# Choice, flag and mask for one tile at a time, and recurrent products in half arrays, in a two-layer kernel with top-k dropping

## The reference

```python
# first layer, main branch
s = silu(einsum('bsh,ih->bsi', xn, w_gate))            # i: 1376
k = int(0.5 * I)                                       # 688
_, idx = top_k(-abs(s), k)                             # the 688 smallest |s| of a token
s = s.at[rows, idx].set(0.0)
s = s * einsum('bsh,ih->bsi', xn, w_up)
s = einsum('bsi,hi->bsh', s, w_down)
# first layer, gate branch: weights quantized to -1, 0, 1 by 0.7 of the row's mean |w|
g = silu(xn @ q_weight.T + bias)

# second layer, main branch: width 64, feed forward 256, depth 4
h = einsum('blv,dv->bld', xn, Win) + bin
for l in range(4):
    y = silu(layernorm(h, ln1_w, ln1_b))
    y = sconv(y, phz, lc)          # y_t = Re(sum_j p^j x_{t-j} + lc p^(t+1)), one complex p per channel
    h = h + y * sc_lin
    y = layernorm(h, ln2_w, ln2_b)
    h = h + silu(y @ w1.T + b1) @ w2.T + b2
s = layernorm(h, lnl_w, lnl_b) @ Wout.T + bout
# second layer, gate branch: x @ W.T plus 16 experts of rank 16, weighted
```

## Time and profile before

| | |
|---|---|
| time, median of 3 runs | 786.28 us (783.88, 789.82, 786.28) |
| the profiled execution | 782.56 us |
| its span in the trace | 780.6 us |
| TensorE busy | 665.8 us, 85% |
| VectorE busy | 513.9 us, 66% |
| ScalarE busy | 324.8 us, 42% |
| GpSimd busy | 241.5 us, 31% |
| mean granted TensorE clock | 0.927 |

### The profile page before, as it was taken

One profiled execution on the slowest core, in us unless ns is written; L12 is line 12 of the kernel. 1 busy time (PEld: TensorE's weight loads), 2 busy tenths in 40 slices (PEclk: granted clock), 3 DMA queues, 4 the chain that ended last, 5 costly groups with the idle time before them and its releaser, 6 DMA issues. The chain is left out here.

```text
span 780.6 us, 8884 instructions
## 1 busy us (share of the span) xinstructions
PE 665.8 (85%) x2724; PEld 475.7 (61%) x2724; DVE 513.9 (66%) x885; ACT 324.8 (42%) x537; POOL 241.5 (31%) x351
## 2 busy tenths in 40 slices
PE   2975898998998998998998987865979699596887
PEld 2764787887887887887887873743434244233443
DVE  6688596585685775865966862947472844727627
ACT  5467285184283373472672562112124133151320
POOL 1000001010010010010010063883346576685756
PEclk9997999999999999999999997985999789799889
DMA  7711001102002002002001080010000000000005
GB/s 265 245 45 55 0 1 46 36 1 78 3 0 81 0 0 81 0 0 81 0 0 55 2 283 28 0 42 0 15 0 13 0 0 13 0 0 13 0 0 216
DMA packets 19209, 33.16 MB, mean 42 GB/s; under 512 B 5008, under 2 KB 5520, under 8 KB 19184
## 3 DMA queue, kind: packets, MB, share of 16 engines
q1 hardware_dynamic: 19184, 32.87, 12.5%
HBM read 25.52 MB, written 7.34 MB: 42 GB/s over the span
## 5 line engine op out<-in xcount | busy, mean ns | idle before, releaser
L743 DVE TENSOR_SCALAR_CACHE_REDUCE junk_d<-k_buf,cand 128x1376 int8<-128x1376 f32 x56 | 91.8, 1640 | 0.3
L582 ACT ACTIVATE junk_a<-k_buf,cand 128x1376 int8<-128x1376 f32 x56 | 80.5, 1437 | 0.7
L979 PE MATMUL ps_a<-wd_hi,zt_hi 128*128 128x512 f32 (+1 forms) x176 | 72.0, 409 | 1.3 <-DVE zt_lo L856 1.0
L502 POOL TENSOR_TENSOR xres<-xres,gate 128x512 f32<-128x512 f32 x12 | 23.5, 1959 | 159.4 <-DVE gate L863 159.4
L954 PE MATMUL ps_a<-wg_hi,xt_hi 128*128 128x512 f32 (+1 forms) x192 | 54.9, 397 | 20.6 <-DVE gate L863 15.7
L979 PE MATMUL ps_a<-wd_hi,zt_lo 128*128 128x512 f32 (+1 forms) x176 | 69.1, 393 | 0.0
L979 PE MATMUL ps_a<-wd_lo,zt_hi 128*128 128x512 f32 (+1 forms) x176 | 69.0, 392 | 0.0
L563 ACT ACTIVATE s_buf<-ps_a 128x1376 f32<-128x1376 f32 x16 | 21.1, 1320 | 110.9 <-DVE m_buf L848 57.5
L1561 PE MATMUL ps_t<-arena 128*128 128x512 f32 x128 | 65.7, 644 | 0.0
L954 PEld LDWEIGHTS ps_a<-wg_hi,xt_hi 128*128 128x128 f32 x192 | 36.3, 201 | 28.6 <-DVE gate L863 14.2
L954 PE MATMUL ps_a<-wg_hi,xt_lo 128*128 128x512 f32 (+1 forms) x192 | 53.3, 388 | 0.0
(11 more groups left out here) (197 smaller groups left out, 1463.9 us busy)
## 6 DMA issues: line engine op xcount, KB each, us to landing
xin<-in_x SPq DMA_DIRECT2D x8, 512.0 KB, 4.0
xres<-in_x SPq DMA_DIRECT2D x8, 512.0 KB, 3.8
out<-arena SPq DMA_DIRECT2D x16, 256.0 KB, 2.3
x_scratch<-xres SPq DMA_DIRECT2D x6, 512.0 KB, 3.0
arena<-x_scratch SPq DMA_DIRECT2D x3, 1024.0 KB, 11.7
m_buf<-in_wd_t SPq DMA_DIRECT2D x3, 512.0 KB, 4.7
m_buf<-in_wg_t SPq DMA_DIRECT2D x2, 688.0 KB, 8.4
k_buf<-in_wg_t SPq DMA_DIRECT2D x2, 688.0 KB, 10.8
```

The lines of the kernel that those rows point to most:

```text
L502: pool.tensor_tensor(row, xres[:, t, :], gate2[:, t, :], ALU.add).then_inc(x1_ready, 1)
L582: act.activation(junk_a[:], k_buf[:, 1, :], ACT.Sign, bias=c, scale=-1.0, accum_out=below[:, 1:2]).then_inc(act_step, 1)
L743: dve.tensor_scalar(junk_d[:], k_buf[:, 0, :], c, -float(DROP), ALU.is_lt, ALU.add, accum_out=e).then_inc(cnt_dve, 1)
L979: last = pe.matmul(ps_a[:, t, :], zs, ws[0:rows, c, :], start=(c == 0 and n == 0), stop=(c == CHUNKS - 1 and n == 2))
```

## The change

Three things change together.

- **By tile.** `choose`, the flag's sum, the load of it, `exact_choice` and `mask` are done for one tile at a time. A choice is eleven steps on one column or 8 columns. The step that added two flags is gone; VectorE loads the summed flag itself. GpSimd does a residual and a sum, and again a residual and a sum.
- **Order on VectorE at a pair's end.** Before: `xt_low` 0, `largest_under` 1, `down_gate` 1, choice of both, `q_bias`, `xt_low` 1, flag, masks of both. Now: choice 0, `xt_low` 0, `down_gate` 1, `largest_under` 1, `q_bias`, mask 0, choice 1, `xt_low` 1; mask 1 stands behind the first two search steps of the next pair, ahead of its first `product`.
- **Second layer.** The padded arrays are gone: `win`, `w1`, `w2`, `wout` hold the weights alone, `w1` and `wout` once for each half of the partitions. Up and output products read 64 rows (sequence b's); `down_unit` and the `win` product write 64 rows of the output, one sequence each. Units go sequence by sequence (b = u % 2), in another order in `layer`, and the first up products of the second half stand ahead of the last down products of the first. `centered` is gone from VectorE: ScalarE squares straight from the bank and then copies to `xc`. The output tiles go in another order (`OUT`).

```diff
-PICKS = 12
+PICKS = 11
...
-                def residual(p, resident=False):
-
-                    for t in range(2):
-                        if t == 0:
-                            pool.wait_ge(x_res, 16 * p)
-                        pool.wait_ge(down_out, 2 * (p - 1) + t + 1)
-                        row = x1[:, 2 * (p - 1) + t, :] if resident else xres[:, t, :]
-                        pool.tensor_tensor(row, xres[:, t, :], gate2[:, t, :], ALU.add).then_inc(x1_ready, 1)
...
+                def residual(p, t, resident=False):
+
+                    if t == 0:
+                        pool.wait_ge(x_res, 16 * p)
+                    pool.wait_ge(down_out, 2 * (p - 1) + t + 1)
+                    row = x1[:, 2 * (p - 1) + t, :] if resident else xres[:, t, :]
+                    pool.tensor_tensor(row, xres[:, t, :], gate2[:, t, :], ALU.add).then_inc(x1_ready, 1)
+
+                def check_sum(p, t):
+
+                    pool.wait_ge(picked, PICKS * (2 * p + t + 1))
                     settled(pool, pool_passed)
-                    pool.partition_all_reduce(bad_all[:], bad[:], P, RADD).then_inc(bad_sum, 1)
+                    pool.partition_all_reduce(bad_all[:, t:t + 1], bad[:, t:t + 1], P, RADD).then_inc(bad_sum, 1)
...
-                check_sum(0)
+                check_sum(0, 0)
+                check_sum(0, 1)
                 with pool.Fori(1, PAIRS - 1) as p:
                     root(p + 1)
-                    residual(p)
-                    check_sum(p)
-
-                pool.wait_ge(up_done, TILES)
-                pool.memset(win, 0.0).then_inc(win_zero, 1)
+                    for t in range(2):
+                        residual(p, t)
+                        check_sum(p, t)
+
                 tables_start(pool)
...
-                residual(PAIRS - 1, resident=True)
-                check_sum(PAIRS - 1)
+                for t in range(2):
+                    residual(PAIRS - 1, t, resident=True)
+                    check_sum(PAIRS - 1, t)
                 tables_powers(pool, 0, 3, DOUBLINGS)
                 tables_powers(pool, 1, 0, DOUBLINGS - 1)
-                residual(PAIRS, resident=True)
+                for t in range(2):
+                    residual(PAIRS, t, resident=True)
...
-                    between()
-                    dve.wait_ge(bad_sum, p + 1)
-                    step(dve.tensor_tensor(bad_int[:, 0:1], bad_all[:, 0:1], bad_all[:, 1:2], ALU.add))
+
+                def mask(p, t):
+
+                    dve.wait_ge(bad_sum, 2 * p + t + 1)
                     settled(dve, dve_passed)
-                    failed = dve.value_load(bad_int[0:1, 0:1], min_val=0, max_val=2 * P)
+                    failed = dve.value_load(bad_all[0:1, t:t + 1].bitcast(I32), min_val=0, max_val=0x44000000)
                     with dve.If(failed > 0):
-                        exact_choice()
+                        exact_choice(t)
+                    dve.wait_ge(z_ready, 2 * p + t + 1)
+                    dve.scalar_tensor_tensor(out=m_buf[:, t, 0:INNER], in0=k_buf[:, t, :],
+                                             scalar=tau[:, t:t + 1], in1=s_buf[:, t, :],
+                                             op0=ALU.is_gt, op1=ALU.mult).then_inc(mask_ready, 1)
...
                     halve(p, 1)
+                    if back:
+                        mask(p - 1, 1)
                     product(p, 0)
...
+                    choose(p, 0)
                     if ahead:
                         xt_low(p + 1, 0)
-                    largest_under(p, 1, back)
                     if back:
                         down_gate(p, 1)
-
-                    def meanwhile():
-                        if first:
-                            dve.wait_ge(bias_in, 16)
-                        for t in range(2):
-                            q_bias(p, t, back)
-                        if ahead:
-                            xt_low(p + 1, 1)
-
-                    choose(p, meanwhile)
-                    mask(p)
+                    largest_under(p, 1, back)
+                    if first:
+                        dve.wait_ge(bias_in, 16)
+                    for t in range(2):
+                        q_bias(p, t, back)
+                    mask(p, 0)
+                    choose(p, 1)
+                    if ahead:
+                        xt_low(p + 1, 1)
...
                 def squares(q, c):
-                    act.wait_ge(ln_xc, 2 * q + c + 1)
-                    act.activation(sq[:, cs(c)], xc[:, cs(c)], ACT.Square).then_inc(ln_sq, 1)
+                    act.wait_ge(ln_cent, 2 * q + c + 1)
+                    act.activation(sq[:, cs(c)], bank1[c], ACT.Square).then_inc(ln_sq, 1)
+                    act.activation(xc[:, cs(c)], bank1[c], ACT.Copy).then_inc(ln_xc, 1)
...
-                        for b in range(BATCH):
-                            for k in range(KH):
-                                last = pe.matmul(bank1[c], win[:, b, k, :],
+                        for k in range(KH):
+                            for b in range(BATCH):
+                                last = pe.matmul(bank1[c][b * DIM:(b + 1) * DIM, :], win[:, k, :],
                                                  xt[:, k, b * SEQ + c * NB:b * SEQ + (c + 1) * NB],
-                                                 start=(b == 0 and k == 0), stop=(b == 1 and k == KH - 1))
+                                                 start=(k == 0), stop=(k == KH - 1))
...
-                    pe.matmul(bankx[u % 2], w1[:, b, m * P:(m + 1) * P], y[:, cs(c)],
+                    pe.matmul(bankx[u % 2], w1[rows, m * P:(m + 1) * P], y[rows, cs(c)],
                               start=True, stop=True).then_inc(f_full, 1)
...
-                    last = pe.matmul(bank1[c], w2[:, b, m, :], hs[:, u, :], start=(u == 0), stop=(u == 3))
+                    last = pe.matmul(bank1[c][b * DIM:(b + 1) * DIM, :], w2[:, m, :], hs[:, u, :],
+                                     start=(m == 0), stop=(m == 1))
```

More of the change, by code:

```diff
@@ L795, in choose @@
[L795 removed]
+                    rank_t, tau_t, above_t, bad_t = (x[:, t:t + 1] for x in (rank, tau, above, bad))
+                    pick_t, top_t = pick[:, t, :], top8[:, t, :]
+                    dve.wait_ge(at_ready, 2 * p + t + 1)
+                    dve.wait_ge(top_ready, 2 * p + t + 1)
+                    step(dve.tensor_scalar(rank_t, at_most[:, t:t + 1], 0.5, 0.25, ALU.mult, ALU.add))
+                    step(dve.tensor_scalar(pick_t, iota8[:], rank_t, None, ALU.subtract))
@@ L1150, in mixture_kernel @@
             FF = 2 * 4
-            OUT = [4 * g + j for g in ORDER for j in range(4)]
+            OUT = [8 * b + j for j in range(8) for b in range(BATCH)]
             def on_pool(m):
```

183 lines of the change are left out of this document (81 added, 102 removed).

## The result

The changed kernel takes 793.3 us in the median of 18 runs (787.08 to 798.72), the kernel before 785.15 (779.32 to 790.06): a ratio of 1.0096, 95% interval 1.0071 to 1.0121. It is slower by 1%, which is clear of the noise, and 801 was forecast: slower by 2%. The profiled execution took 790.37 us, its span is 788.5, 7.9 more than before.

The account below looks back on a forecast made before the run. TensorE was taken to bound the first half, delayed by waits for down_gate. 782.56 us + 27 for the first layer - 12 for the second = 797.6, with 3.7 to the median 801; range 787 to 819.

Parts of the forecast that it names:

- +18: End of the first layer, bound by GpSimd: 120.7 us behind the last pair's start against 102.7, through added code changes.
- +2.0 a pair: First layer's loop: two sums for one delay the up product; a pair goes from 56.4 to 58.4 us, five periods +10.
- before the second pair, down_gate ahead: First layer's start: the first pair's xt_low comes 1.8 us later, the next pair's waits of 2.22 and 0.3 go; -0.7.
- feed forward of four layers: Second layer: half arrays partly overlap, second half bound by ScalarE; -1.8 us a layer, -7 in all.
- win products: Second layer: 16 passes of the second half, 9.08 us, take nine steps, 5.1 us; -4.
- last norm and outputs: Second layer: squares from PSUM take the 0.7 us copy out of the chain only in the last norm; -0.7.
- start of block b: Second layer's start: w1, w2 and wout no longer cleared, which stood beside the wait for VectorE's norms; no gain counted.
- (1): Rival, second layer: the array halves do not overlap, or drains eat the gain; +14, 815 us; chance 0.22.
- (2): Rival, GpSimd in the first layer: change back costs little or is not between sum and second residual; 757 us; chance 0.05.
- (3): Rival: code changes at their short end, 6.1 us, TensorE's own path binds, all of the overlap; 791 us; chance 0.18.
- The drain: Second layer: tiling mode changes about six times a layer, each may drain TensorE; 1.6 us a layer, a reservation.
- The naive reading of down_gate: down_gate alone moved ahead: 2.6 us wait and 1 us low clock go in six pairs, nothing replaces them; -21, 764 us.

## Why the prediction was right and wrong

The direction and the mechanism were right: a change back to plain code between the first sum and the second residual, the wait of the up product, the longer end of the first layer, the gain of the half arrays. What failed is the size of the two terms of the first layer that decide. "+18" for its end measured +14.0: the change to the sum was put at 7.1 us (6.9 at the end), "the longest of the three", and took 5.8 to 6.4 in pairs 1 to 7. "+2.0 a pair" measured +1.4: the 0.4 a pair added because VectorE would lose its lead did not arise. These two make 7.2 of the 7.7 us by which the sum, 15.6 over the span of before, exceeds the measured 7.9. The other five terms miss by 0.4 to 2.4 us each and nearly cancel, and that they do is luck. Each term, with what the two traces give:

| term | predicted | measured |
|---|---|---|
| before the second pair, down_gate ahead | -0.7 | -3.1 |
| five periods | +10 | +6.8 |
| end of the first layer | +18 | +14.0 |
| feed forward of four layers | -7 | -6.1 |
| win products | -4 | -5.4 |
| last norm and outputs | -0.7 | -0.3 |
| start of block b | 0 | +2.0 |
| together | +15.6 | +7.9 |

**The second pair** (-0.7). I charged xt_low of the first pair 1.8 us for the choice ahead of it. It came at 72.80 against 71.50, and TensorE's gate product at 73.55 against 72.81, only 0.7 later. From there to the gate product of tile 1 it is 15.07 us against 18.00, as both waits are gone, and from that one to the second pair's 37.03 against 37.98; I had nothing for the last. The gate product of the second pair's tile 0 stands at 125.65, and could stand at 128.79 before.

**The periods** (+2.0 a pair, measured +1.4). The size "I take 7.1, the longest of the three" was too large: in the changed kernel the twelve sums of pairs 1 to 6 stand 6.0 to 6.4 behind their flags. q_bias was thus done 11.1 us behind the pair's start and not 12.2, and the wait is 3.4 to 4.0 and not 4.7. In the period this shows little, since I took 29.0 for the second up product where TensorE's own path gave 29.4; it started at 28.8 in the mean of five, with a low clock that cost 0 to 2.6 us (1.6 in the mean, 1.5 charged). What was too much is the slack of VectorE, for which I added 0.4: the rest of a period is 28.9 us and was 29.1, and the view of waits has no wait at the second up product.

**The end** (+18, measured +14.0: 102.7 to 116.7 us behind the last pair's start). The change to the sum again: 5.82 where I had 6.9, and 6.15 behind the second flag where I had 7.1; what lies ahead of that flag took 0.5 less, so that from the residual to the second sum it is 11.1 and not 12.6. The table's start 454.59 is 40.3 behind the pair's start, 41.1 was predicted, and the rest of the tables with the residuals took 23.0 and not 23.4.

**The second layer** (-12, measured -9.7). For win I took nine steps out of the 9.08 of the earlier trace rows, 0.32 us a pass, without its granted clock of 0.78; at 1.00 that is 0.25, and 0.23 was measured. So the overlap is little better than my middle value, and the larger gain is the clock, by luck: the same sixteen passes took 5.45 us in the run with the second layer alone. The feed forward is bound by ScalarE as predicted. What is missing is the last line but one of the table. I put the clearing of w1, w2 and wout at nothing "beside the wait for VectorE's norms", and did not ask what GpSimd's next work, now 2.2 us earlier, would meet. That the earlier passes make the 2.0 us is argued from where they fall, not shown: of the kernels whose passes start 5.75 us behind block b's start, six have 32.3 us up to the second win products and one has 30.9, while of three where it is 7.94, two have 30.3 and 30.6 and one has 33.2. What the meeting costs in all is shown: holding the passes back until VectorE is through shortens the stretch by 10 us and the kernel by 7.6.

The Trainium skill, SBUF — State Buffer, SBUF: two separate sides, says that VectorE and GpSimd share one pair of ports under an exclusive lock, taken by a VectorE operation in a 2-port mode, or with two SBUF inputs against a GpSimd operation that reads SBUF, and that whoever comes second waits for the whole instruction. The trace agrees: the steps end within 0.02 us of GpSimd's passes, and fall from 1.88 and 2.29 to 0.16 when the passes are moved. The prediction priced the clearing as time of GpSimd and not by what it delayed.

**The rivals.** (1), no overlap, is refuted by the win products. The run with sequences not alternating costs 9.7 us where 14 was predicted, but it is not (1) as a whole, since its win products still gain and a part of its loss is clock. The drain, for which I kept a reservation, does not show as such: the down and up products of the feed forward change between rows and columns, and four down passes still take 1.03. (2), a cheap change back, is refuted as a description of the chip (6.75 to 7.25 in the loop) and confirmed as a mechanism: without changes the kernel takes 732 us. I had 757 for it, since I let the end of the first layer cost 4 more than before, and it costs 15 less (87.5 us). (3), the changes at their short end, gave 791 and is what happened: changes to the sum at 6.1, TensorE's own path binding in the loop. It had 0.18 and deserved more: three sums of before read 6.1, 6.6 and 7.1, and I took the largest where the middle one would have given about 796. Yet all seven sums of before that follow their flag stand 6.1 to 7.6 behind it, 6.8 in the mean; what 7.1 missed is mostly that the change is shorter in the changed kernel. The estimate from the Trainium skill, GPSIMD Engine Reference, Instruction dispatch, 6 us for a load of code, was nearer than my choice for the change to the sum, and not for the change back.

**The naive reading of down_gate** was half right. In the full change it took away 2.6 us a pair, and the code change put 3.4 to 4.0 in its place. Alone it gains 13 us: the wait of 2.6 with its low clock gives way to one of 1.0 to 1.7 at a granted clock of 1.00, and not of 3 as I had expected, because the flags are ready 1.3 us sooner behind the pair's start.

What stays open: why a change to the sum takes 6.0 to 6.4 us in pairs 1 to 6 of the changed kernel and 6.1 to 7.6 in the kernel before. In the loop before, a residual ended 1.9 us ahead of the flag, and in the changed kernel GpSimd had been idle for some 5; with down_gate ahead the residual ended 2.9 us ahead of the flag, and the change took 6.8 to 7.2. A longer rest ahead of the flag thus goes with a shorter change, but not everywhere: the first sum of the changed kernel stands 6.9 behind its flag after a rest of 15.7. No run varied it alone.

## What to carry to other kernels

A custom operation on GpSimd costs little in itself (0.4 us) and some 13 us in two code changes if plain operations stand around it: count the changes, not the operations, put custom operations next to each other, and look at who is queued behind them. A flag that is needed on one partition can come from TensorE for 0.35 us. A clearing or a copy that is "hidden" sets when the engine's next work starts; before it is put at nothing, ask what that work will meet on other engines. A row of TensorE's time is read with the granted clock beside it before a saving is worked out from it.

## What the hardware showed that I had not expected

- A memset on GpSimd right behind a custom operation needs no code change: it starts as soon as TensorE releases it (446.00 before, 448.38 with the first layer alone), and the change comes behind it, 7.11 and 7.70 us to the first plain operation.
- Products of 64 columns in different halves of the array overlap almost wholly in float32: 0.23 us for a pass of 512 columns, against 0.44 in the full array and 0.34 when all passes of one half come first, each from sixteen win passes at a granted clock of 1.00.
- VectorE's steps on four elements took up to 2.29 us beside GpSimd's passes of 1.95 to 2.34, and 0.16 without them.
- The granted clock was 0.50 to 0.64 behind TensorE's waits of 3.45 to 3.95 us in five pairs of the changed kernel, and 1.00 behind the sixth, of 3.39; in the kernel before, in the 3.5 us behind six waits of 2.59 to 2.70, it was 0.54, 0.70, 0.57, 0.68, 1.00 and 0.66. The length of the wait alone does not tell what it will be.
